# A two-layer decoder on one core: split dependency chains, and two pairs of score banks for the last batch

## Time and profile before

| | us |
|---|---|
| median of 3 runs | 1204.82 (1204.47 to 1206.35) |
| the profiled execution, own time | 1203.95 |
| its span (first to last instruction) | 1202.2 |
| PE busy | 1076.3 (90%) |
| DVE busy | 1021.4 (85%) |
| ACT busy | 761.0 (63%) |
| POOL busy | 197.5 (16%) |

### The profile page before, as it was taken

How to read it: one execution, slowest core, us unless ns; L and a number is a source line. 1 busy time by engine, 2 the same in 40 slices (tenths; PEclk the granted TensorE clock), 3 DMA queues, 4 the chain that set the end, 5 groups by cost and what they waited for, 6 DMA issues and landing times.

```text
span 1202.2 us, 17418 instructions
## 1 busy us (share of the span) xinstructions
PE 1076.3 (90%) x6154; PEld 796.0 (66%) x6154; DVE 1021.4 (85%) x1690; ACT 761.0 (63%) x2010; POOL 197.5 (16%) x257
## 2 busy tenths in 40 slices
PE   5665789898999999999999999999998999999884
PEld 3444556674778677766776688757875887677663
DVE  3999989999999999999999999998999984433316
ACT  4544435677667866787678866885677656536534
POOL 0000110021221213131313031213131311010002
PEclk8766769999999999999999999999999999999997
DMA  6431111123334233423343234313441320000302
GB/s 221 147 117 59 35 51 37 54 53 71 72 81 109 62 72 71 124 66 72 70 108 82 57 77 103 86 39 60 97 121 28 82 58 23 1 1 10 138 1 70
DMA packets 41193, 86.70 MB, mean 72 GB/s; under 512 B 3737, under 2 KB 14970, under 8 KB 40466
## 3 DMA queue, kind: packets, MB, share of 16 engines
q1 hardware_dynamic: 27282, 60.42, 15.8%
q0 software_dynamic: 13824, 25.17, 12.1%
HBM read 54.38 MB, written 6.04 MB: 50 GB/s over the span
## 4 chain that ended last, share of the span: by engine, by line
PE 56%; DVE 28%; ACT 7%; issue 6%; POOL 2%; DMA 1%; ACTq 0%; DVEq 0%; SPq 0%; POOLq 0%
PE bank L292 17%; DVE scans L576 8%; DVE scans L584 4%; PE bank L1245 4%; PE bank L1201 4%; PE bank L737 4%; PE bank L927 3%; PE bank L921 3%; PE bank L512 3%; PE bank L1143 3%; PE bank L1234 2%; PE bank L1210 2%; PE bank L692 2%; DVE conv L431 2%; DVE nmax L1336 2%
## 5 line engine op out<-in xcount | busy, mean ns | idle before, releaser
L541 ACT ACTIVATE scans<-dt,a_neg 128x255 f32<-128x255 f32 x512 | 225.4, 504 | 0.1
L609 POOL DMA_DIRECT2D scans<-scans x96 | 84.7, 886 | 437.4 <-DVE scans L584 436.7
L584 DVE TENSOR_TENSOR scans<-scans,BC 128x1024 f32<-128x1024 f32 x128 | 155.9, 1218 | 0.0
L1282 ACT ACTIVATE ya<-bank,nmax 128x256 f32<-128x256 f32 x256 | 118.4, 475 | 54.5 <-DVE nmax L1336 26.3
L576 DVE TENSOR_TENSOR_SCAN scans<-scans,dBx_odd 128x1024 f32<-128x1024 f32 x64 | 146.3, 2286 | 2.0 <-ACT scans L541 2.0
L576 DVE TENSOR_TENSOR_SCAN scans<-scans 128x1024 f32<-128x1024 f32 x64 | 146.2, 2284 | 0.8 <-ACT scans L538 0.6
L512 PE MATMUL bank<-ident,scans 128*128 128x128 f32 x640 | 103.1, 300 | 28.9 <-DVE scans L584 24.6
L512 PEld LDWEIGHTS bank<-ident,scans 128*128 128x128 f32 x640 | 83.6, 155 | 52.2 <-DVE scans L584 30.1
L1336 DVE TENSOR_REDUCE nmax<-bank 128x2 f32<-128x512 f32 x128 | 83.8, 684 | 28.2 <-PE bank L1201 28.1
L1289 ACT ACTIVATE ya<-bank 128x512 f32<-128x512 f32 x128 | 74.2, 603 | 19.1 <-PE bank L1210 13.3
L538 ACT ACTIVATE scans<-neghalf 128x4 f32<-128x4 f32 x128 | 27.0, 211 | 92.1 <-PE bank L512 91.9
(11 more groups left out here) (267 smaller groups left out, 2244.3 us busy)
## 6 DMA issues: line engine op xcount, KB each, us to landing
BC<-xpj_scratch SPq DMA_DIRECT2D x31, 1024.0 KB, 5.9
scans<-scans POOLq DMA_DIRECT2D x96, 256.0 KB, 3.3
xin<-in_x SPq DMA_DIRECT2D x8, 256.0 KB, 3.1
conv<-in_x SPq DMA_DIRECT2D x8, 256.0 KB, 2.8
out<-scans SPq DMA_DIRECT2D x8, 256.0 KB, 2.1
kept_x<-x SPq DMA_DIRECT2D x7, 256.0 KB, 3.0
kept_w<-wa SPq DMA_DIRECT2D x7, 256.0 KB, 2.0
BC<-kept_w SPq DMA_DIRECT2D x1, 1792.0 KB, 9.0
```

What stands on the lines that cost most here:

```text
L541: ins = act.activation(step[:, j, 1:S], dt[b % 2][:, c, 1:S], ACT.Exp, scale=a_neg[:, c, n:n + 1])
L584: dve.tensor_tensor(H, H, Ch, ALU.mult).then_inc(s["a_hC"], 1)
L1282: act.activation(pe_[:, h % 2, t, :], YB[h % 2][:, t * S:(t + 1) * S], ACT.Exp, bias=nmax[:, h % 4, t:t + 1], accum_out=ls[:, p % 2, t, h ...
```

## The change

**More places to yield.** `stats_end` and `stats` become generators with a `yield` ahead of each wait, and so do the links in `x_dve`, `z_dve`, `v_dve`, `gate_dve` and `front_dve`; what was `own.link(...)` becomes `own.did(...)`, `yield`, `own.wait()`. On ScalarE and TensorE many two-part steps get a `yield` between the parts. No instruction is added or taken away there.

```diff
-        def stats_end(dve, own, st, tag):
+        def stats_end(dve, own, st, tag, done):
+            yield
             own.wait()
             for t in range(T):
                 own.did(dve.bn_aggr(ln_mv[tag][:, t, :], ln_sts[st][:, t, :]))
+            yield
             own.wait()
             own.did(dve.tensor_scalar(ln_nm[tag][:, :], ln_mv[tag][:, :, 0], -1.0, None, ALU.mult))
-            return dve.tensor_scalar(ln_var[tag][:, :], ln_mv[tag][:, :, 1], EPS, None, ALU.add)
+            dve.tensor_scalar(ln_var[tag][:, :], ln_mv[tag][:, :, 1], EPS, None, ALU.add).then_inc(done, 1)
...
                     if k < TAPS - 2:
+                        yield
                         own.wait()
...
-            own.link(dve.tensor_tensor(ahead, ahead, tie.rearrange("p (e j) -> p e j", e=NE).unsqueeze(1).to_broadcast(pairs), ALU.is_gt))
-            own.link(dve.tensor_reduce(rank, ahead, AX, ALU.add))
+            own.did(dve.tensor_tensor(ahead, ahead, tie.rearrange("p (e j) -> p e j", e=NE).unsqueeze(1).to_broadcast(pairs), ALU.is_gt))
+            yield
+            own.wait()
+            own.did(dve.tensor_reduce(rank, ahead, AX, ALU.add))
+            yield
...
-            own.link(dve.scalar_tensor_tensor(flat(ug[:, 1, :, :]), flat(tg[:, 1, :, :]), 1.0, flat(tg[:, 2, :, :]), ALU.add, ALU.mult))
+            own.did(dve.scalar_tensor_tensor(flat(ug[:, 1, :, :]), flat(tg[:, 1, :, :]), 1.0, flat(tg[:, 2, :, :]), ALU.add, ALU.mult))
+            yield
+            own.wait()
             dve.scalar_tensor_tensor(flat(state[:, :, :]), flat(ug[:, 0, :, :]), 0.5, flat(ug[:, 1, :, :]), ALU.mult, ALU.add).then_inc(s["l_state"], 1)
...
             def recur(g, bk):
                 for m in range(KD):
+                    if m:
+                        yield
                     for k in range(KD):
...
```

```diff
+        ahead_pe, ahead_pT = [dt[i][:, :, :].rearrange("p (j a) s -> p j a s", j=2) for i in range(2)]
+
+        def ahead(b, h):
+            return b == NB - 1 and (h // 2) % 2 == 1
+
+        def score_bank(b, h):
+            return SA[h % 2] if ahead(b, h) else YB[h % 2]
...
+        def pairs_done(b, p):
+            return p - 1 if b == NB - 1 else p
...
             def scores(p):
                 g = 2 * p // GH
-                if p:
-                    pe.wait_ge(*of("t_pT", b, 2 * p))
+                if pairs_done(b, p) > 0:
+                    pe.wait_ge(*of("t_pT", b, 2 * pairs_done(b, p)))
+                if b == NB - 1 and p == 1:
+                    pe.wait_ge(*of("a_res", b))
...
             for p in range(NQ // 2):
-                scores(p)
-                yield
+                if b < NB - 1 or p == 0:
+                    scores(p)
+                    yield
+                if b == NB - 1 and p < NQ // 2 - 1:
+                    scores(p + 1)
+                    yield
                 turned(2 * p)
                 yield
                 turned(2 * p + 1)
```

**New orders.** All five strings are new; a line of VectorE's:

```diff
-        "WYVYYVYWYYYVWWWVVWWWVYYYYYYYWYYYWWVYYYVYYYYVYYVWYYYYWVWYYYVYYYVVVVWWWWWWWWWWWW"
+        "VVVVYYYVYYVYYYYYYWYVYWWWYWWWWYYYWVYYYYYVYYYVYYYYVWYVWYVWWWWVVVVVVVVVWWWWWWWWWWWWWWWWWW"
```

More of the change, by code:

```diff
@@ L422, in front_dve @@
             dve.wait_ge(*of("a_x", b))
-            stats(dve, own, xin, "f", "a").then_inc(s["a_var"], 1)
+            yield from stats(dve, own, xin, "f", "a", s["a_var"])
             yield
@@ L601, in gate_dve @@
                     yield
-            stats_end(dve, own, "s", "a1").then_inc(s["a1_var"], 1)
+            yield from stats_end(dve, own, "s", "a1", s["a1_var"])
             yield
@@ L874, in x_dve @@
                     yield
-            stats_end(dve, own, "w", "f1").then_inc(s["x_var"], 1)
+            yield from stats_end(dve, own, "w", "f1", s["x_var"])
             yield
@@ L967, in z_pe @@
                 pe.wait_ge(*of("a_res", b))
+                pe.wait_ge(*of("t_pT", b))
                 kept_product(pe, 6)
@@ L1238, in v_pe @@
             for p in range(NQ // 2):
-                values(p)
+                yield from values(p)
                 yield
@@ L1271, in y_act, with powers @@
                 yield
-            for p in range(NQ // 2):
+            def powers(p):
                 if p >= 2:
@@ L1329, in y_dve, with greatest @@
                 yield
-            for p in range(NQ // 2):
+            def greatest(p):
                 for h in (2 * p, 2 * p + 1):
@@ L1355, in v_dve @@
                 dve.wait_ge(*of("t_out_ps", b, t + 1))
-                own.link(dve.tensor_tensor(x3[b % 2][:, t, :], [y1, y2][t][:, 0:D], x3[b % 2][:, t, :], ALU.add))
+                own.did(dve.tensor_tensor(x3[b % 2][:, t, :], [y1, y2][t][:, 0:D], x3[b % 2][:, t, :], ALU.add))
+                yield
+                own.wait()
                 stats_of(dve, own, x3[b % 2], "y", t)
@@ L1359, in v_dve @@
                     yield
-            stats_end(dve, own, "y", "t1").then_inc(s["t_var"], 1)
+            yield from stats_end(dve, own, "y", "t1", s["t_var"])
+            yield
             dve.wait_ge(*of("t_var", b, 1))
@@ L1364, in v_dve @@
                 dve.wait_ge(*of("t_rstd", b - 1))
-            own.link(dve.reciprocal(ln_var["c"][:, :], ln_var["t1"][:, :]))
+            own.did(dve.reciprocal(ln_var["c"][:, :], ln_var["t1"][:, :]))
+            yield
+            own.wait()
             dve.tensor_scalar(ln_var["c"][:, :], ln_var["c"][:, :], -EPS, 1.0 + EPS, ALU.mult, ALU.add).then_inc(s["t_var"], 1)
```

220 lines of the change are left out of this document (159 added, 61 removed).

## The result

Eleven runs of each kernel, taken in turns: 1199.11 us after (1194.84 to 1203.41) against 1204.82 before (1203.71 to 1207.02). The ratio is 0.994, interval 0.9927 to 0.9954, so 7.2 us faster by the ratio (5.5 to 8.8) and 5.7 by the medians. Forecast were 19.3 (the sum's 1185.8 had been put down as 1185.5). The sign was right, the size was not, and the time is rival A's, 1198.8. The runs in which the experiments were measured had the kernel before with them again, and its executions spread there from 1203.2 to 1210.7 us, so ratios are used, each to the kernel before of its own runs. The profiled execution took 1199.11 us, its span 1197.2.

A forecast was written before the change was run, and what follows sets the result against it. VectorE was taken to bound the scans' stretch, two thirds of the span. From the profiled 1203.95 us, 13 (VectorE's chains) and 6 (last attention) came off; with 0.87 for the median 1185.8, put down as 1185.5, range 1177 to 1193.

The forecast's parts named there:

- rival A: VectorE gains nothing because TensorE hands the 13 us back; only the tail's 6 us arrive: 1198.8 us, chance 0.11.
- VectorE's chains: Ahead of the last scan, 157 fewer instructions wait for the one directly ahead, 0.12 us each: 18.8 us, 13 counted.
- I take 70% of it: Share of VectorE's 18.8 us expected to arrive, since denser orders leave less time for other engines' answers: 13 us.
- So two thirds of the span go at VectorE's pace: From 186 to 984 us VectorE is busy 97.4% and was taken to set the pace.
- The last batch's attention: From 1083 to 1137 us a second pair of banks fills TensorE's 7.6 us of waits: 6 us, lasting 47 to 49.
- ScalarE's and TensorE's yields at nothing: New places to part two-part steps add no instruction; delays below 1.2 us each, costed at nothing.
- C: W stream's serial line becomes the bound, its links lengthened by instructions put between: slower, 1212.8 us, chance 0.13.
- The signs named: Right: last scan near 971 us, attention 47 to 49 us. Wrong: last scan at 984 or later, or attention of 54.

The follow-up runs named there:

- e6a: Changed kernel with an added wait on VectorE itself at every second product, 57 more waiting neighbours: 1196.34 us, 0.9911 of the kernel before.
- e10a: Changed kernel, five layernorms a batch (third to seventh) normalised by constants on ScalarE without waiting for GpSimd: 1187.9 us, 0.9843 of the kernel before.
- e1: Old orders up to the last batch's attention, then the changed kernel's tail with the second pair of score banks: 1198.65 us, 0.9943 of the kernel before.
- v2: Changed kernel's orders up to the 40th scan, old orders behind, then the new tail with the second pair: 1202.11 us, 0.9953 of the kernel before.
- e2: New orders up to the last batch's attention, then the old order without the second pair of score banks: 1203.81 us, 0.9975 of the kernel before.
- e3a: Changed kernel with 15 us of VectorE products left out: 0.9934 of the kernel before, 0.7 us faster than the changed kernel.
- e5a: Changed kernel with 17.3 us of the W stream's feed-forward matmuls on TensorE left out: 0.9936 of the kernel before.
- e4a: Changed kernel with 19.6 us of TensorE's sums over states left out, third to seventh batch: 0.9897 of the kernel before.
- e9a: Changed kernel with the VectorE cut of e3a and the TensorE cut of e4a together, 34.6 us: 0.9857 of the kernel before.
- e12: Changed kernel, constants without GpSimd's wait only for layernorms behind the Mamba block and self-attention, third to seventh batch: 1191.2 us, 0.9876 of the kernel before.
- e11: Changed kernel, constants without GpSimd's wait only for the W stream's three layernorms, third to seventh batch: 1193.15 us, 0.9888 of the kernel before.
- e8: Kernel before with only 44 of the scans' plain products moved forward into gaps in VectorE's order: 1241.26 us, 1.0279 of the kernel before.
- e6b: Kernel before with an added wait on VectorE itself at every second product, 58 more waiting neighbours: 1208.9 us, 1.0034 of the kernel before.
- e3b: Kernel before with 15 us of VectorE products left out: 0.9954 of the kernel before, 5.5 us faster.
- e4b: Kernel before with 19.6 us of TensorE's sums over states left out, third to seventh batch: 0.9985 of the kernel before, 1.8 us faster.
- e10b: Kernel before, five layernorms a batch (third to seventh) normalised by constants without waiting for GpSimd: 1205.09 us, 0.9987 of the kernel before.
- e7: Kernel before with 198 instructions moved forward by one to three places in VectorE's order: 1356.95 us, 1.1247 of the kernel before.

## Why the links bind now

GpSimd's product takes 0.20 us by itself. Around 323 us in the kernel before it stands beside a residual that reads a bank (start us, us):

```profile
323.57 0.69 POOL L275 TENSOR_TENSOR rstd_c<-var_c,neghalf 128x2 f32<-128x2 f32 x1 [1.24 <-DVE var_c L267]
324.00 0.42 DVE L1356 TENSOR_TENSOR x<-bank,x 128x256 f32<-128x256 f32 x1
324.34 0.20 POOL L276 TENSOR_TENSOR shift_c<-minus_c,rstd_c 128x2 f32<-128x2 f32 x1
...
324.57 0.99 ACT L279 ACTIVATE cz<-cz,shift_c,rstd_c 128x192 f32<-128x192 f32 x2 [0.31 <-POOL shift_c L276]
324.80 2.27 DVE L576 TENSOR_TENSOR_SCAN scans<-scans 128x1024 f32<-128x1024 f32 x1
```

The same place in the changed kernel:

```profile
320.31 0.69 POOL L284 TENSOR_TENSOR rstd_c<-var_c,neghalf 128x2 f32<-128x2 f32 x1 [1.59 <-DVE var_c L276]
...
321.06 2.29 DVE L598 TENSOR_TENSOR_SCAN scans<-scans 128x1024 f32<-128x1024 f32 x1
321.07 2.26 POOL L285 TENSOR_TENSOR shift_c<-minus_c,rstd_c 128x2 f32<-128x2 f32 x1
...
323.37 0.98 ACT L288 ACTIVATE cz<-cz,shift_c,rstd_c 128x192 f32<-128x192 f32 x2 [2.10 <-POOL shift_c L285]
```

The scan starts 0.01 us ahead of the product and ends at 323.35; the product ends at 323.33, 2.26 us for 0.20, and ScalarE waits 2.10. This has a rule in the Trainium skill, page "SBUF — State Buffer", section "Who interferes with whom": a VectorE instruction with two inputs in SBUF shuts out a GpSimd instruction that reads SBUF until it is done. The trace agrees here. Between 186 us and the last scan 102 small GpSimd instructions run, of which 24 take longer than 0.8 us before and 27 after; 3 of these end together with a scan before and 11 after. From the start of the inverse root to the end of the product, 42 layernorms take 64.0 us before and 76.7 after; 7 and 17 of them are longer than 2 us. So the new orders, which put another instruction directly behind a link, often put a scan there, and the hop becomes longer by 12.7 us in all.

One place shows what such a hop does, and that it isn't all, batch 7's feed-forward. At scan 112 the changed kernel leads by 3.4 us, at 116 by 3.9, at scan 120 by nothing. The rows between (start us, us):

```profile
896.06 0.16 DVE L276 TENSOR_SCALAR var_b<-mv_b 128x2 f32<-128x2 f32 x1
897.05 2.28 DVE L598 TENSOR_TENSOR_SCAN scans<-scans 128x1024 f32<-128x1024 f32 x1
897.06 2.26 POOL L285 TENSOR_TENSOR shift_b<-minus_b,rstd_b 128x2 f32<-128x2 f32 x1
899.36 1.09 ACT L288 ACTIVATE xb<-xb,shift_b,rstd_b 128x256 f32<-128x256 f32 x2 [2.44 <-POOL shift_b L285]
900.01 0.93 PE L295 MATMUL bank<-ident,xb 128*128 128x128 f32 x4 [1.60 <-ACT xb L288]
904.62 0.19 DVE L865 COPY low<-bank 128x32 f32<-128x32 f32 x1 [3.57 <-PE bank L301]
```

The busy time of the same stretch, columns as in the earlier trace rows:

```profile
896.00:900.00 4.00, 1.72 (x16) 1.13 (x16) 4.00 (x8) 1.56 (x5) 3.63 (x3) 1.00 0.00 0
900.00:904.00 4.00, 3.93 (x19) 2.41 (x19) 1.05 (x1) 3.13 (x9) 0.17 (x1) 0.63 0.38 66
904.00:908.00 4.00, 4.00 (x8) 1.89 (x9) 3.31 (x15) 1.12 (x5) 0.75 (x1) 0.52 0.00 0
```

The scan holds GpSimd, GpSimd holds ScalarE, ScalarE holds TensorE, which is busy 1.72 of 4 us. Behind that the granted clock is 0.63 and 0.52, that is at 1.2 GHz for the larger part of 8 us, and VectorE stands 3.57 us until the router's first product is there. The variance is followed by `low` 904.62 - 896.06 = 8.6 us later.

But the kernel before has the same hop at the same place:

```profile
899.93 0.16 DVE L267 TENSOR_SCALAR var_b<-mv_b 128x2 f32<-128x2 f32 x1
900.97 2.29 POOL L276 TENSOR_TENSOR shift_b<-minus_b,rstd_b 128x2 f32<-128x2 f32 x1
900.99 2.28 DVE L576 TENSOR_TENSOR_SCAN scans<-scans 128x1024 f32<-128x1024 f32 x1
907.19 0.18 DVE L829 COPY low<-bank 128x32 f32<-128x32 f32 x1
```

And e6a, with the orders of the changed kernel, has the hop and no fall of the clock:

```profile
894.31 0.16 DVE L276 TENSOR_SCALAR var_b<-mv_b 128x2 f32<-128x2 f32 x1
895.32 2.26 POOL L285 TENSOR_TENSOR shift_b<-minus_b,rstd_b 128x2 f32<-128x2 f32 x1
901.25 0.19 DVE L866 COPY low<-bank 128x32 f32<-128x32 f32 x1 [1.94 <-PE bank L301]
```

Its busy time there, as above:

```profile
894.00:898.00 4.00, 1.72 (x16) 1.13 (x16) 4.00 (x9) 1.46 (x4) 3.37 (x3) 1.00 0.02 8
898.00:902.00 4.00, 3.67 (x22) 2.27 (x23) 2.06 (x5) 3.28 (x10) 0.43 (x1) 1.00 0.38 66
```

From the variance to `low` it is 7.3 us in the kernel before and 6.9 in e6a. In e10a it is 5.0 us:

```profile
890.34 0.16 DVE L276 TENSOR_SCALAR var_b<-mv_b 128x2 f32<-128x2 f32 x1
891.09 0.72 ACT L294 ACTIVATE xb<-xb 128x256 f32<-128x256 f32 x2
891.34 2.28 DVE L604 TENSOR_TENSOR_SCAN scans<-scans 128x1024 f32<-128x1024 f32 x1
891.35 2.26 POOL L285 TENSOR_TENSOR shift_b<-minus_b,rstd_b 128x2 f32<-128x2 f32 x1
895.33 0.19 DVE L871 COPY low<-bank 128x32 f32<-128x32 f32 x1
```

GpSimd is held there as well, 2.26 us, and nobody waits for it; the granted clock stays at 1.00 from 884 to 912 us. Runs side by side at this place:

| run | product on GpSimd | variance to `low` | clock, scans 116 to 120 | scans 116 to 120 |
|---|---|---|---|---|
| before, e1 | 2.29 us | 7.2 to 7.3 us | 1.00 | 30.2 us |
| v2 (old orders here) | 2.29 | 8.4 | 0.90 | 33.2 |
| changed kernel, e2, e3a, e5a | 2.26 | 8.0 to 8.8 | 0.90 | 34.0 to 34.2 |
| e4a, e6a, e9a, e12 | 2.26 | 6.9 to 7.0 | 1.00 | 31.0 to 31.1 |
| e10a, e11 (not waited for) | 2.26 | 5.0 | 1.00 | 29.1 |

So of the 4.0 us by which the changed kernel is slower here, 3.1 go with the fall of the clock and 0.9 with the orders; taking the hop out of the link gives 2.0 more. Why the clock fell in one execution and not in the other is open: TensorE was busy 1.72 us of the 4 ahead in both.

The place where the gain on VectorE really goes is earlier, and there the clock is 1.00 in both kernels. From scan 40 to scan 92 the changed kernel takes 411.6 us, the kernel before 403.7; the lead turns from 5.6 us to -2.3. e10a takes 404.5, with one fall of the clock (574 to 577 us). So 7.1 of the 7.8 us come back when the normalisations don't wait for GpSimd (and are shorter on ScalarE). Behind that the lead grows by 4.0 us from scan 104 to 108, where the kernel before has a fall of the clock (816 to 820 us), and shrinks by 3.9 from 116 to 120, where the changed kernel has its own.

How the missing gain divides isn't settled. e10a's 11.7 us come from 25 hops and include some 3 us of the fall at 900, which leaves 8.6. At the mean of 1.83 us the hops are 46 us of link, and the shorter normalisations make it 55; 8.6 / 55 is 0.16 us of time for each. By that the hops' 12.7 us would cost some 2 us, an estimate. The rest I put down to links that end later by the instruction placed in them, as in e8, and to TensorE's slower stretches; that is argued from e8 and these rows, and no run parts the three. A kernel with the new orders that only keeps scans away from the hops was not tried.

## Why the prediction was wrong, step by step

- **"VectorE's chains".** The price of a wait was right, 0.12 us: 157 x 0.12 = 18.8 us forecast up to the last scan, 11.2 us less busy time from 186 us on and 12.6 us by the waits from 180 to 950 us; e6b confirms from the other side that waits cost time (4.1 us for 7.0). The Trainium skill, page "VectorE: DVE Perf Modes", section "The DRAIN you can't avoid", says that a semaphore after each of eight copies cost nothing extra. The starts of the earlier trace rows, 0.13 us apart with and without the wait, and e6b disagree; the measurement decides.
- **The step that failed is "I take 70% of it".** It made 13 us of the 18.8. About 3.0 us arrived by e2 (1.3 to 4.7), 16%, and 0.8 us by the last scan in e2's trace. The 70% rested on idle time in sums: 36.3 us on TensorE, 229 on ScalarE. But slack counted over a stretch isn't slack where a link needs it. I said that denser orders leave less time for the answers, and then priced it at 30% with no row behind it.
- **"So two thirds of the span go at VectorE's pace"** was too strong, and the error lay in reading 97.4% busy as a bound. e3b took 15 us off VectorE and got 5.5. e4b and e10b got 1.8 and 1.6 us from the same kernel, so no one of the three, VectorE, TensorE or the links, is the bound there alone.
- **GpSimd was never costed.** It was busy 164.80 of 798 us and seemed free. Its hop lies in every layernorm's link, and its length depends on which VectorE instruction stands beside it.
- **The last batch's attention: the waits right, the size near.** 6 us forecast, 47 to 49 us long; measured 6.9 us alone (e1, 4.3 to 9.4) and 48.6 us. By the traces it is less: 4.3 us from the last scan to the end, and 2.3 of the 5.2 us by which the attention got shorter is work that moved behind it. ScalarE did not become the bound.
- **ScalarE's and TensorE's yields at nothing:** not told apart from the orders.
- **Rivals.** A had the right time, but only in part the right reason: TensorE doesn't hand the gain back by its amount of work alone (e4a gives 5.2 of 19.6 us). Its "against" had the waits too high as well: of the 13 us in that view 11.5 are for TensorE. C's mechanism, links lengthened by what is put between them, is the one that the runs support for the loss (e10a against e10b, scans 40 to 92); it was wrong in laying it on the W stream alone (e11 against e12) and in its price, since it ate the gain and no more. Its "against" compared VectorE's 0.69 us and places in the order, and left out the other engines of the link.
- **The signs named** were the right ones: a last scan at 984 with new idle time on VectorE that TensorE ends was to mean A or C, and that is what the profile shows.

## What to carry to other kernels

When a kernel's streams answer each other across engines, price a reordering by its links: for each one, producer's end to consumer's start, before and after, with every engine of the hop, the small ones too. A busy share of 97% doesn't say that work taken away will arrive; take a little away, or shorten one link without taking work away, and see which of the two the time follows. Before a loss at one place is put down to a wait there, look for the same wait in the kernel before, and at TensorE's granted clock in both. Two parts of a change are worth running apart early: here one carried all of it.

## What the runs showed of the hardware

- A GpSimd instruction of 128x2 takes 0.20 us, and 2.26 to 2.29 us when a VectorE scan of 128x1024 starts within 0.02 us of it; the two end within 0.02 us of each other.
- A VectorE instruction that waits for the one directly ahead starts 0.03 to 0.04 us after its end, an independent one 0.08 to 0.10 us before it. 58 added waits cost the kernel before 4.1 us (e6b).
- 44 products of 1.2 us moved forward into chains of the old order cost 32.8 us by the last scan (e8), and 198 moves by one to three places 152 us of run time (e7), where the largest saving in sight was 23 us.
- A normalisation of 128x256 on ScalarE takes 0.59 us with scale and bias from tiles and 0.41 us with constants (e10a).
- TensorE's granted clock fell to 0.52 behind 4 us in which it was busy 1.72 us; in e6a it stayed at 1.00 behind 4 us with the same 1.72. Scans 116 to 120 took 34.2 us with the fall and 31.1 without, and e6a's last scan came at 979.0 instead of 983.7. The changed kernel's runs spread over 8.6 us; that such stretches are the cause is likely but wasn't shown, and the kernel before spread over 3.3 us beside it and over 6 to 7 us in later runs.
